# A two-layer graph network on one core: TensorE's work inside a group in another order, state rows loaded ahead of the attributes, and one pause of GpSimd in place of two

## The reference, cut to what matters

```python
h = relu(layernorm(x))
xp = (h @ W).reshape(n, 4, 32)                       # layer 1
e = leaky_relu(a_s[src] + a_d[dst], 0.2)             # one logit per edge and head, with self loops
e = exp(e - segment_max(e, dst)[dst])
alpha = e / segment_sum(e, dst)[dst]
x = x + relu(segment_sum(alpha * xp[src], dst) + bias)

h = relu(layernorm(x))                               # layer 2
edge_agg = segment_sum(edge_attr @ We + be, dst)
x_comb = concatenate([h, edge_agg])
neigh = segment_sum(x_comb[src], dst)
x = x + relu((x_comb + neigh) @ W1 + b1) @ W2 + b2
```

## Time and profile before

| | us |
|---|---|
| median of 3 runs | 3248.04 (3247.97 to 3249.55) |
| the profiled execution, its own time | 3249.53 |
| its span in the profile | 3247.6 |
| PE busy | 2133.8 (66%) |
| DVE busy | 1838.2 (57%) |
| POOL busy | 1516.2 (47%) |
| ACT busy | 1095.0 (34%) |

### The profile page before, as it was taken

One profiled execution on the slowest core, in us unless ns is written; L12 is line 12 of the kernel. 1 busy time (PEld: TensorE's weight loads), 2 busy tenths in 40 slices (PEclk: granted clock), 3 DMA queues, 4 the chain that ended last, 5 costly groups with the idle time before them and its releaser, 6 DMA issues.

```text
span 3247.6 us, 60418 instructions
## 1 busy us (share of the span) xinstructions
PE 2133.8 (66%) x16302; PEld 1640.0 (50%) x16302; DVE 1838.2 (57%) x6265; ACT 1095.0 (34%) x2343; POOL 1516.2 (47%) x1625
## 2 busy tenths in 40 slices
PE   4466665665666666656666676666676676667987
PEld 3354554554554545545445454454454445455766
DVE  7365666666666666656556565555555556564221
ACT  3333333333333344333333333333333233332000
POOL 3555555555555555554545555445444444550000
PEclk8666766766767766778878788788888788878999
DMA  9845545555555555565555655556555555655665
GB/s 195 121 137 163 167 139 163 155 153 162 155 153 163 148 165 172 152 182 150 179 153 174 173 170 180 149 162 177 159 153 176 166 147 172 180 138 189 209 198 159
DMA packets 395176, 532.44 MB, mean 164 GB/s; under 512 B 115603, under 2 KB 346723, under 8 KB 383665
## 3 DMA queue, kind: packets, MB, share of 16 engines
q1 hardware_dynamic: 344939, 415.35, 42.4%
q0 software_dynamic: 50112, 115.56, 15.9%
HBM read 385.48 MB, written 145.24 MB: 163 GB/s over the span
## 4 chain that ended last, share of the span: by engine, by line
PE 26%; DVE 21%; another core or an unknown queue 21%; issue 13%; DMA 8%; ACT 5%; SPq 5%; ACTq 1%; DVEq 1%
PE pv L1352 9%; PE pv L1284 5%; PE pt L1275 4%; ACT xsb L942 4%; DVE tabb L1640 4%; DMA state<-zpart 4%; DMA state<-sums 3%; PE pt L1253 2%; DVE big L1932 2%; PE pv L1409 2%; DVE lks L1915 1%; DVE fy L1759 1%; DVE fy L1768 1%; PE pt L1409 1%
## 5 line engine op out<-in xcount | busy, mean ns | idle before, releaser
L906 POOL DMA_INDIRECT big<-table,idx x1566 | 1489.2, 951 | 1372.4 <-issue 399.2
L942 ACT ACTIVATE xsb<-pt 128x343 f32 x1042 | 482.0, 463 | 1547.7 <-remote 922.0
L1253 PE MATMUL pt<-tabb 128*128 128x343 bf16 x1042 | 379.5, 364 | 448.1 <-ACT xsb L942 405.8
L1284 PE MATMUL pv<-big 128*128 128x128 f32 x3132 | 511.3, 329 | 8.0 <-issue 5.6
L1284 PEld LDWEIGHTS pv<-big 128*128 128x128 f32 x3132 | 476.3, 239 | 32.2 <-issue 13.7
L1352 PE MATMUL pv<-big 128*128 128x133 f32 x3132 | 391.6, 280 | 22.2 <-DVE big L1932 22.2
L1253 PEld LDWEIGHTS pt<-tabb 128*128 128x128 bf16 x1042 | 107.9, 104 | 553.8 <-ACT xsb L942 439.9
L1352 PEld LDWEIGHTS pv<-big 128*128 128x128 f32 x3132 | 367.9, 190 | 35.5 <-DVE big L1932 22.4
L1640 DVE TENSOR_TENSOR tabb<-pc,keyp 128x2064 bf16<-128x2064 bf16 x261 | 319.0, 1222 | 0.0
L942 ACT ACTIVATE xsb<-pa 128x343 f32 x521 | 240.9, 462 | 61.8
L1932 DVE TENSOR_TENSOR big<-big,pm 128x768 f32<-128x768 f32 x261 | 233.4, 950 | 30.8 <-ACT pm L942 19.0
(11 more groups left out here) (339 smaller groups left out, 3282.5 us busy)
## 6 DMA issues: line engine op xcount, KB each, us to landing
adj<-xsb SPq DMA_DIRECT2D x87, 1176.0 KB
big<-in_edge_attr_dram SPq DMA_DIRECT2D x87, 1152.0 KB
selb<-rel SPq DMA_DIRECT2D x87, 576.0 KB
...
```

What stands on the lines that cost most here:

```text
L906: pool.indirect_dma_start(out=V[b][:, j, 0:rows], out_offset=None, in_=table, in_offset=bass.IndirectOffsetOnAxis(ap=index[b][:, j:j + 1], ...
L942: return nc.scalar.activation(out_, in_, func, **kw).then_inc(s(name), 1)
L1253: ins = nc.tensor.matmul(to, ohl[:, c, :], ohk[:, c, 0:KW], start=True, stop=alone)
L1284: ins = nc.tensor.matmul(sumA[b], SEL[b][:, j, :], AT[b][:, j, :], start=(j == 0), stop=(j == J - 1))
```

## The change

- **Order of TensorE.** Adjacency chunks 9 to 14 of a group, which stood at the end of its item, move into the next item behind `cback`; chunks 15 to 17, which stood there, move behind mg; chunks 0 to 2 of the group itself move from behind mg to behind look; chunks 3 to 5 move behind all attribute sums. Six attribute sums instead of three stand ahead of look in plain groups, none in job groups (`LEAD`). The job is one piece, between mg and look. The projection of a window moves from inside `sumV` to the start of the next item.
- **ScalarE** makes the selection copy directly behind `thruT`, ahead of all chunks; chunks 9 to 17 of group n-1 follow it, chunks 0 to 2 of n come behind `normalise_window`, 3 to 8 at the item's end.
- **VectorE** rescales the state behind the scan of the tails, reads the job's result behind the edge marks (ahead of the wait for look), and takes the projection on another signal.
- **SP** loads the state rows and stores the residual ahead of loading the attributes.
- **GpSimd** stops once, ahead of gather 10, for look.

The core of the diff:

```diff
-FILL = (10, 14)
-PAUSES = ((11, "mg_b"), (14, "look"))
+PAUSES = ((10, "look"),)
+LEAD = (6, 0)
...
                 load_job(n, like)
-                if ahead is not None:
-                    load_attributes(n + 2, b, ahead)
                 if before_first:
                     sp.wait_ge(s("tab_out"), 32 * (TAB_CHUNKS + 1))
                 load_sums(n, base)
                 if not before_first:
                     store_residual(n - 1, base_before)
+                if ahead is not None:
+                    load_attributes(n + 2, b, ahead)
...
                 a(thruT[:, :], thruP, ACT.Copy, "thru_c")
-                if finish_before:
-                    keep_adjacency(n - 1, 1 - b, 15, 18)
...
                 a(SEL[b], selH, ACT.Copy, "selc_b")
-                if not is_extra:
-                    after_dma(act, s("adj_out"), n - 1)
-                    keep_adjacency(n, b, 0, 3)
-                else:
+                if finish_before:
+                    keep_adjacency(n - 1, 1 - b, 9, 18)
+                if is_extra:
...
                 if not is_extra:
-                    keep_adjacency(n, b, 3, 6)
+                    after_dma(act, s("adj_out"), n - 1)
+                    keep_adjacency(n, b, 0, 3)
...
-                    keep_adjacency(n, b, 6, 15)
+                    keep_adjacency(n, b, 3, 9)
...
-                job(n, like, 0, FILL[0])
+                if finish_before and not (isinstance(n, int) and n < 2):
+                    project_window(n - 2)
                 after(pe, s("pre1_b"), n)
                 after(pe, s("thru_c"), n)
                 nc.tensor.transpose(tailT, pre1[:, :, J - 1], ident[:, :]).then_inc(s("tailT_b"), 1)
-                job(n, like, FILL[0], FILL[1])
...
                 if finish_before:
-                    adjacency(n - 1, 15, 18)
+                    adjacency(n - 1, 9, 15)
...
-                job(n, like, FILL[1], NB)
...
                 ins.then_inc(s("mg_b"), 1)
-                if not is_extra:
-                    adjacency(n, 0, 3, like)
+                if finish_before:
+                    adjacency(n - 1, 15, 18)
...
-                attribute_sums(0, 3)
+                lead = LEAD[1 if parts_of(like) else 0]
+                attribute_sums(0, lead)
+                job(n, like)
...
                 ins.then_inc(s("look"), 1)
                 if not is_extra:
+                    adjacency(n, 0, 3, like)
+                attribute_sums(lead, J)
+                if not is_extra:
                     adjacency(n, 3, 6)
-                attribute_sums(3, J)
...
                 for q in range(QN):
-                    if q == QN - 1 and finish_before:
-                        project_window(n - 1)
...
                 ins.then_inc(s("vm_b"), 1)
-                if not is_extra:
-                    adjacency(n, 9, 15)
...
                 select(n, b, extra_group)
-                if m is not None:
-                    rescale_state(m, 1 - b)
...
                 if m is not None:
+                    rescale_state(m, 1 - b)
                     add_sums(m, 1 - b)
...
-                keep_job(n, like)
                 after(dve, s("mg_b"), n)
...
                 if not is_extra:
                     edge_marks(n, 1)
+                    keep_job(n, like)
```

37 lines of the change are left out of this document (17 added, 20 removed).

## The result

The change makes the kernel slower by 23%: 3983.11 us, the median of four runs (3974.12 to 4000.75), against 3248.8 for the kernel before beside it; ratio 1.227, 95% interval 1.224 to 1.229. The profiled execution took 4000.75 us, span 3998.9.

What follows compares the result with a forecast made beforehand. Bound by a chain through several engines, much of it late signals. 41 plain cycles at -1.1 us (-45) and jobs +14 sum to -31 us: 3218.5 us against the profiled 3249.5, 3217 against the median; range 3055 to 3335.

Steps and rivals of the forecast that it cites:

- GpSimd, one pause: GpSimd's gathers: one run of 18, as the sums end at about +9.8; gain 1.1 us in each plain cycle.
- Selection copy first, chunks 9 to 17 moved: ScalarE and TensorE order: sums end somewhat later than +9.8; covered until +10.8, each us beyond costs one per plain cycle.
- the hold: Between engines: results are held while a stream of gathers runs; mg read 3.25 us after the last gather started.
- Attributes behind the state rows ... nothing by itself: SP's queue: attributes start about when the sums end, as before, and are needed a group later; no cost by itself.
- wait (a): DVE, logit to tails: 6.42 us where group 0 needs 1.79; DVE idle 4.24 us before rescaling state rows; removed.
- The logit comes later: DVE reads the logit at +12.4 instead of +8.5; costs nothing until about +15.3.
- first rival: Slower: gathers 16 and 17 land late beside attributes and adjacency, logit to +16.7; 3312 us, upper end 3386; chance 0.26.
- The job in one piece: TensorE between mg and look: 28 job matmuls take 6.2 us, bounds 4.5 to 8.7; jobs add 14 us in all.
- mg and look: DVE's reading in plain cycles: mg 0.3 us earlier; look without gathers takes 2.3 us instead of 3.12, gain 0.8.
- wait (c): DVE reads look 3.12 us after its start, with gathers 11 to 13 under way; 1.47 in group 39.

Runs made afterwards that it cites:

- e7: Changed kernel with chunks 3 to 5 back where they stood on TensorE and ScalarE: 3641.28 us, ratio 1.116 to the kernel before (late chip, kernel before 3267 us).
- e8: Changed kernel with chunks 3 to 5 back and the projected window stored ahead of the attributes: 3639.00 us, ratio 1.115 (late chip).
- e10: Changed kernel with chunks 3 to 5 back, window stored first, and gather 4 also waiting for mg: 3300.37 us, ratio 1.010 (late chip).
- e16: Changed kernel with waits ahead of gathers 5 and 14 until earlier gathers landed: 3309.57 us, ratio 1.260 (prompt chip, kernel before 2627 us).
- e17: Changed kernel with waits ahead of gathers 5 and 14 until earlier gathers landed: 3475.73 us, ratio 1.070 (late chip, kernel before 3250 us).
- e9: Kernel before with gather 8 waiting for mg and gather 11 for look, instead of 11 and 14: 3224.90 us, ratio 0.986 (late chip).
- e2: Changed kernel with the projected window stored ahead of loading the attributes: 2871.66 us, ratio 1.092 (prompt chip, kernel before 2627 us).
- e3: Kernel before with only the one new pause, gather 10 waiting for look: 2656.02 us, ratio 1.011 (prompt chip).
- e14: Kernel before with only the one new pause, gather 10 waiting for look, measured again: 2653.09 us, ratio 1.011 (prompt chip).
- e4: Kernel before with gather 9 waiting for mg and gather 12 for look, instead of 11 and 14: 2622.55 us, ratio 0.999 (prompt chip).

## Why the prediction was wrong

Forecast 3217 us and a range up to 3335; measured 3983. By its own steps:

- **GpSimd, one pause.** Forecast one run of 18 gathers, a gain of 1.1 us. There is none: eight gathers, 11.18 us of waiting, ten gathers. The eight set off right (+0.75, last start +9.49), but the sums were not done at +9.8; they ended at +20.8. The step rested on the sums staying where they were.
- **"Selection copy first, chunks 9 to 17 moved"** is the step that failed. I wrote that TensorE's chunk 8 stands ahead of the sums and that they "end somewhat later", with a cover of 1 us, and put no size on it. Measured, the sums end at +18.8 in plain groups and at +22.2 with 28 job matmuls (medians), 8 to 11 us beyond the +10.8 that the cover allowed. I did not follow ScalarE's order: exponentials, then the copy of the transposes, then chunks 3 to 5. Those three chunks now wait for a result of TensorE, and so do the sums. Undone, it gives 455 us (e7, on a late chip). Of the later start, 4.2 us are there on a prompt chip too; the rest comes with the hold.
- **The hold was seen, and not applied.** I read it in mg, look and carry, and let it gain 1.1 us there. The same reading says that a run of eight behind look holds the transposes at +4.5 until it ends. Put to them, with the 1.08 us that I had read at the carry, it gives ScalarE's copy at +10.6, the three chunks behind it and the sums from about +13, and the other sign. The reading itself held, on late chips, as far as results are late while a run goes on (e8, e10 and the pair e16 and e17); that TensorE's own matmuls stop too (e8, e9) was not in it.
- **"Attributes behind the state rows ... nothing by itself"** was the other miss. I asked what stood behind the attributes on the queues (gathers, adjacency), and not which DVE instruction needs the projected window stored: L1774, right ahead of the carry. The state rows were taken out from behind the attributes; the store had stood behind them all along, hidden by the 4.24 us of wait (a), and stayed. The attributes wait for the end of the sums, so load and store moved with it. What was forecast as the removal of wait (a) gave 0.5 us in the group shown (end of the sums to carry 7.4 us, before 7.8), and the other 277 us were there to be had (e2, prompt chip). Wait (a) was also misread: TensorE's transpose for tails started only at 1045.07, so without the state rows tails would have come some 0.6 us earlier, not 4.24.
- **The logit comes later**: +16.65 against +12.4, because the edge marks ahead of it (L1632) wait for chunks of TensorE that are late too, 594.2 us in the waits above. The first rival had the sign but not the mechanism: no late landing set the end.
- **The job in one piece.** 7.06 us for 28 matmuls was forecast as 6.2, bounds 4.5 to 8.7: right. (The prediction's 0.17 us for one at the higher clock stands in no row of it; 14 of them took 2.44 us at 2400.36, 0.174 each, granted clock 1.00.) It starts 1.2 us behind pen and stands on the chain as forecast: pen to mark is 8.5 us with 28 matmuls, before 5.0. What was to pay for it did not come: the carry of these groups was forecast at +23.1 and came at +29.1, as the sums ended late. On a prompt chip, where no carry was late before, the job costs 5.0 us behind pen, 140 us in 28 groups, and saves 0.6 ahead of it. Rows of the changed kernel, TensorE, a job group that takes 43.20 us:

```profile
2438.68 2.44 PE L1269 MATMUL pt<-tabb,pro 128*128 128x384 bf16 x7
...
2445.74 0.60 PE L1325 MATMUL pa<-node,selb 128*128 128x24 bf16 x18
```

- **mg and look.** mg was forecast to be read 3.25 us behind the last gather's start, and nearly is: 1054.90 - 1051.94 = 2.96. Look without gathers beside it was to take 1.5 to 3.1 us; it takes 1059.39 - 1058.67 = 0.72. But wait (c) was misread: before, DVE was busy with the edge marks until 0.74 us ahead of reading look, so most of the 3.12 us was its own work, and now look starts later behind pen (3.77 us, before 1.94). From pen to the mark it is 4.49 us against 5.06: a gain of 0.6 where 0.8 was forecast, for another reason. On prompt chips the old order reads look 1.9 to 2.0 us behind its start even with no gather beside it (e3, e14, plain groups).
- **A slip in rival 1.** Its upper end is added up wrong: 24.6 + 4.46 + 1.94 + 2.3 = +33.3 is 2.6 us more than 30.7, 107 us in 41 cycles and not 124, so about 3370 us and not 3386. It moves nothing.

How the loss divides on a late chip, by what undoing each part gives: three chunks 0.14, the pauses 0.035 to 0.06, the rest of the order about 0.05, the store nothing as long as mg is held anyway. These are gains in this order of undoing, and the parts act on each other: with the pauses left as changed, one more wait for mg takes 0.08 to 0.105 off (e10). On a prompt chip moving the store gives 0.106, the pauses nothing, and 0.09 is left. It was not divided by runs; the profile of e2 has 2.5 us more in a plain cycle than e4 (27.3 against 24.8) and 3.5 more in one with 28 job matmuls (29.1 against 25.6).
